# A two-layer block kernel: the order of PE and SyncE work in its second stretch of expert blocks, and the row numbers of its scatter adds

## The reference, cut to what matters

```python
t = xf * jax.lax.rsqrt(jnp.mean(xf * xf, axis=-1, keepdims=True) + EPS) * norm_w
logits = t @ gate_w.T + gate_b
vals, idx = jax.lax.top_k(logits, TOP_K)
gates_k = jax.nn.softmax(vals, axis=-1)
G = jnp.zeros((M, E), x.dtype).at[jnp.arange(M)[:, None], idx].set(gates_k)
h = jnp.einsum('mh,eoh->emo', t, w1) + b1[:, None, :]
a = jnp.minimum(h[..., ::2], LIMIT)
b = jnp.clip(h[..., 1::2], -LIMIT, LIMIT)
act = a * jax.nn.sigmoid(ALPHA * a) * (b + 1.0)
y = jnp.einsum('emi,edi->emd', act, w2) + b2[:, None, :]
delta = jnp.einsum('me,emd->md', G, y)
return x + delta.reshape(B, S, H)
```

## The kernel before, in words

| stage | engine | what | line |
|---|---|---|---|
| xb | SP | row load, 128 x 529 words, `xsD` to a ring of 11 buffers | L802 |
| w2x | SP | second weights of the block's expert, 256 KB, to a ring of 4 | L811 |
| x_t | PE | two transposes of the rows | L1065 |
| x_out | ACT | their copy out of PSUM | L1348 |
| w_in | ACT | first weights of the expert, scaled by `norm_w`, ring of 2 | L1341 |
| h_mm | PE | h product, 8 matmuls | L1076 |
| e_a, e_b | DVE | bias and clamp | L1757, L1764 |
| e_tanh | ACT | the sigmoid's tanh | L1354 |
| e_g, e_act | DVE | gated product | L1772, L1777 |
| y_mm | PE | y product, 2 matmuls | L1085 |
| y_out | DVE | times gate and gain, to one of 5 buffers `YB` | L1785 |
| tok | POOL | copies the 128 token numbers to a column of `to`, ring of 6 | L1916 |
| y_add | POOL | indirect DMA that adds the 128 rows into DRAM | L1926 |

## Time and profile before

### The profile page before, as it was taken

The page is one execution under the profiler, slowest core; times in us unless marked ns, Lnnn a source line. Parts: engine busy times, 40 slices in busy tenths (PEclk is TensorE's granted clock), DMA queues, the critical chain, the costliest instruction groups (busy, mean ns, idle before and its releaser), DMA issues.

```text
span 1041.7 us, 20507 instructions
## 1 busy us (share of the span) xinstructions
PE 970.5 (93%) x6020; PEld 820.9 (79%) x6020; DVE 722.6 (69%) x2545; ACT 671.3 (64%) x1944; POOL 427.1 (41%) x450
## 2 busy tenths in 40 slices
PE   6999999999999999999999999996888799999990
PEld 4669888887988888888888888884677689999980
DVE  3564775777677678677867867776867668888870
ACT  2657786687677767757866776782735456676650
POOL 3322431342362353154236225224064555665673
PEclk9999999999999999999999999998999899999995
DMA  9928993994789210020012004057177699998954
GB/s 307 307 80 301 376 371 113 375 377 164 278 293 376 96 62 1 18 88 31 1 62 73 2 1 165 3 183 264 52 188 169 188 247 217 225 226 215 225 133 81
DMA packets 93725, 180.53 MB, mean 173 GB/s; under 512 B 9949, under 2 KB 29085, under 8 KB 92717
## 3 DMA queue, kind: packets, MB, share of 16 engines
q1 hardware_dynamic: 73467, 148.55, 43.1%
q0 software_dynamic: 18800, 30.30, 12.9%
q10 hardware_dynamic: 1346, 0.36, 0.2%
HBM read 77.71 MB, written 107.99 MB: 178 GB/s over the span
## 4 chain that ended last, share of the span: by engine, by line
PE 86%; DVE 4%; issue 3%; ACT 2%; DMA 2%; POOL 1%; SPq 0%; ACTq 0%; DVEq 0%; POOLq 0%; another core or an unknown queue 0%
PE bank L1076 12%; PE bank L1040 11%; PE bank L1012 10%; PE bank L1085 6%; PE bank L1030 5%; PE bank L1002 5%; PE bank L991 4%; PE bank L962 3%; PE bank L868 3%; PE bank L1031 3%; PE bank L1001 3%; PE bank L1021 3%; PE bank L877 3%; PE bank L946 2%; PE bank L984 2%
## 5 line engine op out<-in xcount | busy, mean ns | idle before, releaser
L1076 PE MATMUL bank<-RB 128*128 128x128 f32 x1264 | 157.8, 279 | 6.1 <-issue 3.8
L1076 PEld LDWEIGHTS bank<-RB 128*128 128x128 f32 x1264 | 150.6, 195 | 9.6 <-issue 4.6
L1871 POOL TENSOR_TENSOR RB<-RB 128x512 f32<-128x512 f32 x64 | 67.6, 1056 | 203.1 <-DVE RB L1650 203.1
L1040 PE MATMUL bank<-RA,RB 128*128 128x256 f32 x512 | 133.7, 383 | 1.1 <-DVE X L1690 0.8
L1341 ACT ACTIVATE RB<-RA,nw 128x512 f32 x158 | 105.5, 715 | 37.2 <-issue 16.5
L1012 PE MATMUL bank<-RA 128*128 128x256 f32 x512 | 121.2, 380 | 0.0
L1012 PEld LDWEIGHTS bank<-RA 128*128 128x128 f32 x512 | 95.2, 190 | 15.0 <-issue 2.9
L1040 PEld LDWEIGHTS bank<-RA,RB 128*128 128x128 f32 x512 | 91.0, 190 | 15.5 <-issue 4.7
L1847 POOL TENSOR_TENSOR qs<-qs,half 128x4 f32<-128x4 f32 x64 | 64.9, 1014 | 93.1 <-DVE qs L1659 79.6
L1085 PE MATMUL bank<-RB,BC 128*128 128x256 f32 x316 | 83.2, 387 | 3.3 <-DVE BC L1777 2.3
L1242 ACT ACTIVATE RB<-bank 128x256 f32<-128x256 f32 x128 | 48.7, 381 | 57.9 <-PE bank L1031 52.8
(11 more groups left out here) (251 smaller groups left out, 2387.3 us busy)
## 6 DMA issues: line engine op xcount, KB each, us to landing
xsD<-BC SPq DMA_DIRECT2D x17, 4232.0 KB, 33.0
RB<-in_w2b SPq DMA_DIRECT2D x79, 256.0 KB
RB<-xsD SPq DMA_DIRECT2D x62, 264.5 KB
BC<-modD SPq DMA_DIRECT2D x16, 512.0 KB, 4.2
X<-xsD SPq DMA_DIRECT2D x17, 264.5 KB, 3.4
RA<-in_w SPq DMA_DIRECT2D x2, 2048.0 KB, 8.0
RA<-in_w SPq DMA_DIRECT2D x6, 512.0 KB, 11.5
RA<-in_L_attn_Wq SPq DMA_DIRECT2D x1, 2048.0 KB, 13.8
```

The source lines that it names most:

```text
L1040: m = pe.matmul(bank[5][:, t * 256:t * 256 + 256], OT[:, u % 2, t * 128:t * 128 + 128], Wo[:, h, :], start=(h == 0 and t == 0), stop=(h == ...
L1076: m = pe.matmul(ps[:, 128 * j:128 * j + 128], WS[:, n % 2, c, 128 * j:128 * j + 128], XT[:, n % 2, c * 128:c * 128 + 128], start=(c == 0), ...
L1871: pool.tensor_tensor(sq, qrow, qrow, ALU.mult).then_inc(mine("q_sq", p), 1)
```

## The change

Four edits, all about the second stretch.

1. The y product of block 21 goes ahead of x_t of block 24 and h_mm of block 23 (it stood behind them). All other y products stay.
2. SP asks for six blocks of rows ahead instead of eight, and sends the first two w2x behind the third and the fourth row load instead of behind all of them.
3. In this stretch there is no tok. The add takes its 128 row numbers from column 256 of the loaded rows, so the ring buffer is in use until the add has landed: xb of block m now waits for y_add of block m-11. The first stretch keeps its tok.
4. merge is two DMAs of 128 x 8 KB instead of four of 64 x 8 KB.

```diff
-    lo, hi, ahead = FIRST, NBLK, 8
+    lo, hi, ahead = FIRST, NBLK, 6
     for n in range(lo, lo + ahead):
         load_block(n)
-    for n in range(lo, lo + 2):
-        p.add("w2x", n, slot=n % 4, by=16)
+        if lo + 2 <= n < lo + 4:
+            p.add("w2x", n - 2, slot=(n - 2) % 4, by=16)
...
-        if lo <= n - 1 < hi:
-            p.add("tok", n - 1)
         if lo <= n < hi:
             p.add("e_g", n)
             p.add("e_act", n)
-        if lo <= n - 2 < hi:
+        if lo < n - 2 < hi:
             p.add("y_mm", n - 2, bank=5 + (n + 1) % 3, first=True)
+        if n == lo + 1:
+            p.add("y_mm", lo, bank=5 + lo % 3, first=True)
...
                     if n >= FIRST + RINGS[1]:
-                        on.wait_ge(*done("y_out", n - RINGS[1]))
-                        on.wait_ge(*done("tok", n - RINGS[1]))
+                        on.wait_ge(*done("y_add", n - RINGS[1]))
...
                 on.wait_ge(*done("y_out", n))
-                on.wait_ge(*done("tok", n))
+                if n < FIRST:
+                    on.wait_ge(*done("tok", n))
+                else:
+                    on.wait_ge(*done("xb", n))
...
-                pool.indirect_dma_start((out_r, accD)[n % 2], bass.IndirectOffsetOnAxis(to[:, n % 6:n % 6 + 1], 0), YB[n % 5], None,
+                places = to[:, n % 6:n % 6 + 1] if n < FIRST else rows(n)[:, 256:257].bitcast(U32)
+                pool.indirect_dma_start((out_r, accD)[n % 2], bass.IndirectOffsetOnAxis(places, 0), YB[n % 5], None,
                                         bounds_check=2047, oob_is_err=False, compute_op=ALU.add).then_inc(mine("y_add", n), 16)
...
-                for i in range(4):
-                    pool.dma_start(out_r[512 * i:512 * i + 512, :].rearrange("(a c) n -> a (c n)", c=8), accD[512 * i:512 * i + 512, :].rearrange("(a c) n -> a (c n)", c=8),
+                for i in range(2):
+                    pool.dma_start(out_r[1024 * i:1024 * i + 1024, :].rearrange("(a c) n -> a (c n)", c=8), accD[1024 * i:1024 * i + 1024, :].rearrange("(a c) n -> a (c n)", c=8),
```

More of the change, by code:

```diff
@@ L500, in lay_out @@
             load_block(n + ahead)
-    p.add("merge", by=16 * 4)
+    p.add("merge", by=16 * 2)
     return p
```

## The result

| | before | changed |
|---|---|---|
| median of the runs | 1045.55 us (1044.02 to 1047.83, 10 runs) | 1049.56 us (1045.45 to 1053.1, 10 runs) |
| profiled execution; its span | 1043.59; 1041.7 | 1049.03; 1047.2 |

Two further studies gave 1.0047 [1.003, 1.0065] and 1.0052 [1.0033, 1.007]. One of the six runs of e8 was in a slow state at 1467.15 us, and its ratio goes by the other five.

The account below looks back on a forecast made before the run. PE was taken to bound the second stretch, and the slightly slower chain of adds its end. Gains of 1.05 us (first y product) and 0.15 us (copies) made -1.2 us, 1045.91 to 1044.7 us, range 1041.9 to 1048.9.

Parts of the forecast that it names:

- six blocks ahead with the new wait: Second stretch's row loads wait for the add eleven blocks before to land; PE may stall late, booked at 0.
- The sign that the prediction had named: Number declared wrong if a table's step at block 49 isn't within 0.04 us of 6.08 over 20 blocks.
- Rival C: Experiments' theory on the second stretch's loads: six blocks ahead are too few; no chance given.
- B: Experiments' rival theory on the adds: offsets read from the loaded rows make them slower; no chance given.
- The slower rival: Adds' step gets longer as landings release adds and loads together: +0.2 us a step, 1048.9 us; chance 0.19.
- The first y product: Start of second stretch: block 21's y product ahead of the third h product fills PE's holes, gaining 1.05 us.
- The weights in turn: SyncE's start of second stretch: first weights become the fourth request, landed before needed; cost nothing.
- Copies gone: POOL's copies between adds removed: 0.04 us for each of four back-to-back last adds, 0.15 us gained.
- Offsets from rows: Adds read 128 offsets from loaded rows with another stride; taken as 0, bounds 0 and 0.8 us an add.
- The merge: Final merge in two DMAs instead of four: bytes bound it, not their number, so taken as 0.
- The rival by the piece: Final merge: each DMA has 2.0 us fixed cost, two fewer give 4.0 us, 1040.7 us in all; chance 0.03.
- The faster rival: Adds' step gets 0.1 us shorter as loads held by adds collide less: -3.2, 1042.7 us; chance 0.33.

Follow-up runs that it names:

- e8: Changed kernel with only a quarter of each second weight loaded in the second stretch (products not the reference's): 1037.63 against 1041.23 us before, ratio 0.9962.
- e9: The changed kernel again, unaltered, second study: median 1049.06 us, ratio 1.0047 to the kernel before.
- e12: Changed kernel with thirteen row buffers instead of eleven, six ahead, second run: 1045.24 us, ratio 1.0004 to the kernel before.
- e16: The changed kernel a third time, unaltered: 1050.25 us, ratio 1.0052 to the kernel before.
- e14: Changed kernel with the copies and the old row-load wait back, six ahead, merge in two, second run: 1045.12 us, ratio 0.9999 to before.
- e4: Changed kernel with thirteen row buffers instead of eleven, first run: 1039.42 us, ratio 0.9987 to the kernel before.
- e11: Changed kernel with thirteen row buffers and eight blocks ahead instead of six: ratio 1.0036 to the kernel before.
- e2: Changed kernel with the copies and the old row-load wait back, six ahead, merge in two, first run: 1039.79 us, ratio 0.9983 to before.
- e3: Changed kernel with adds taking offsets from copies again, row loads still waiting for a landed add: 1043.69 against 1041.93 us before, ratio 1.0030.
- e15: Changed kernel with thirteen row buffers and copies back as offsets, still waiting for a landed add: ratio 1.0009 to the kernel before.
- e1: Kernel before with only the early y product and the weights in turn, first run: 1039.7 against 1041.93 us, ratio 0.9977.
- e13: Kernel before with only the early y product and the weights in turn, second run: 1043.91 against 1045.27 us, ratio 0.9991.
- e10: Changed kernel with the merge in four transfers again: 1049.03 us, ratio 1.0049 to the kernel before.
- e6: Kernel before with only the first y product moved early, weights in their old place: 1044.96 against 1041.23 us, ratio 1.0029.
- e7: Kernel before with early y product, weights in turn and four add tables instead of two (two never merged): 1036.59 against 1041.23 us, ratio 0.9959.

## Why the prediction was wrong, step by step

**The step that failed** is the term that the prediction put at nothing, six blocks ahead with the new wait: "As long as adds trail, such a stall costs nothing at the end, because the adds' chain ends last and not PE. I book 0". In place of 0 the new wait cost 3.8 us (e9 against e12, one chip, two buffers more) to 5.1 us (e16 against e14, one chip, the old wait and the copies back).

The premise held: in the changed kernel the adds do end last. From block 30 on no add started less than 1.8 us after the end of its y_out, where 0.8 is the distance of an add that waits for nothing else; so none of them was waiting for PE's product. The size of the stall was about right too: 4.1 us up to y_out(72), a few tenths of a us a block. The prediction counted rows in time up to a lag of 5.1 us and weights up to 6.0; the lag was 6.1 at block 49 and 8.8 at block 67 (before 6.3 and 6.9), and PE's holes behind loads stand at 959, 978, 1005 and 1011 us.

What does not follow from them is 0. It takes the adds' pace as given, and the same wait changed that pace: a table's step between blocks 29 and 69 went from 5.91 to 6.27 us. Counted on the adds, the changed kernel gains 1.1 us between adds 21 and 29, loses 7.3 in the twenty steps to add 69 and 0.4 from there to add 78, which makes 6.6. Counted on the y_outs the same 6.6 us are 4.1 up to y_out(72) and 2.4 from there to add 78, with a lag of 7.5 at block 72 in place of 4.1. The sign that the prediction had named came: over the first twenty blocks, 29 to 49, the step was (943.06-880.99)/10=6.21, more than 0.04 off 6.08. The adds' pace and PE's stalls have one source, the same landings: each now releases the next add and a row load together, as the chain above shows for add 67.

Most of a lag also reaches the end. It gets shorter once the loads run out and adds land quickly (before from 6.9 us at block 67 to 3.2 at block 74), but the column from y_out(72) to add 78 shows up to 5 us between kernels with no lag and with the longest.

That the wait is the cause is shown by the pair e4 and e12 against the changed kernel (the loss goes when the awaited add is two blocks older), with e11 (it comes back with eight ahead) and e2 and e14 (it goes with the old wait). Rival C, B, the early product and the merge are out by e2 and e11, by e3 and e15, by e1 and e13, and by e10.

**The slower rival** was the right side, and for the reason that it gives. "The landing of an add now releases both the next add and, through SyncE, a row load and a weight load": the step is 6.12 to 6.27 in the seven kernels where a load waits for the add three or five blocks back with full weights, and 5.91 to 6.07 in those with two tables and either no such wait or seven blocks. It was priced at +0.2 us over 6.08, "21*0.2=4.2", and 6.28 is what the step came to (6.27); but the base was off: 6.08 was read from blocks 29 to 49, while up to block 69 before makes 5.91 a step, so that the rise was 0.36. Its mechanism, which the prediction gave 0.19, is what the runs bear out, and PE's stalls showed "too", as it said. Lag, late loads and step seem to feed on each other: in the changed kernel the lag stops growing at some 7 to 9 us (6.9 to 8.8 at block 67 in its three profiles), which fits PE being held by the same landings. e8 shows that the loads beside the adds lengthen the step. How much of the rise from 5.91 to 6.27 is loads at the wrong moment, and how much of the loss would be there if PE had been held and the adds had not, no run separates; that stays open.

**The first y product** was right: h_mm(25) starts at 855.58, where 856.19+0.34 would be its old place, so 0.95 us against 1.05 forecast. The weights in turn cost nothing that shows, and without them PE waits 4.01 us (e6); the text had said that both edits need each other, and that the old place held PE "to nearly 852". It did to 848.76, in a profile whose row loads begin 3.0 us earlier (835.00 against 838.03), so to 851.8 by the clock of before.

**Copies gone** was right in kind: the last adds stand 1.85 us apart instead of 1.88 to 1.93, which is below what can be measured, as is the step of e15 against e4. **Offsets from rows** at 0 holds (e15 against e12). Whether missing copies make the new wait a little worse (e3 with way 162.1 against 162.8 to 164.3) stays open: the intervals overlap.

**The merge** at 0 was right: 17.52 us against 17.72 from its first issue to the end. The rival by the piece falls: e10 against e9 shows 0.2 us. The Trainium skill ("DMA: Bandwidth & Descriptors", "Anatomy of one DMA — SWDGE (gpsimd) path") gives some 2.0 us of fixed cost for one DMA, from which the prediction estimated 4.0 us for two fewer; for these transfers, issued one behind the other on POOL, that cost did not add up by the piece.

**The faster rival** had its mechanism wrong: an even release by adds doesn't make them collide less. Its floor was about right, as e7 and e8 show: from y_out(72) to add 78 they take 15.3 and 15.1 us where before took 17.4, and the prediction had 2.2 less.

Last, the sum of the forecast was made against the adds' chain between blocks 29 and 49, and never asked what the chain does once loads cease, though the earlier trace rows show the last adds 1.9 us apart instead of 3.

## What to carry to other kernels

Before a wait for a landed transfer takes the place of a wait for an engine, count in blocks: the lag of what is awaited, plus its landing, plus everything in order behind the wait, against the depth of the ring less the distance of prefetch. Here five blocks lost 4 us and seven lost nothing, so two more buffers or the old wait are the remedy. And before a wait is booked at nothing because another chain ends last, ask whether the wait changes the pace of that chain: here the adds released the loads, and the loads lay beside the adds. Measure a lag where nothing else is tied to it; the tail behind the last y_out was the same 5.7 to 6.2 us for lags of 3.4 to 7.5 us at block 72, because that y_out waited for an add itself or the adds could not be issued faster.

## What the runs showed of the chip that was not expected

- Indirect accumulating DMAs of 128 rows of 1 KB issued on POOL 1.84 to 1.86 us apart when nothing held them, and 1.87 to 1.93 with the offsets in a small tile (1.91 to 1.93 of these with a copy between). Under loads the step of two alternating tables was 5.9 to 6.3 us, and in e8 it fell to PE's 5.74 when the traffic beside them fell from 219 to 161 GB/s.
- Freed of the copies, POOL's busy time in 870 to 890 us fell from 11.36 to 9.66 us and the DMA share from 0.93 to 0.87, and the kernel was slower. Neither number told whether the kernel would be faster.
- Between two profiles of the same kernel the way from y_out(21) to y_out(78) scattered by up to 2 us (e1 and e13, e4 and e12), with the lag of the adds, while up to y_out(72) it was the same within 0.3 us; in the changed kernel's three profiles it was 150.1 to 150.7.
